# Where the shared expert's two halves run, and in which PSUM banks, in an attention and mixture-of-experts kernel

## The chip, the cores and the metric

One Trainium2 chip, one of its cores. The metric is the device time of one execution in microseconds; lower is better. Times of the kernel before: median 366.74 us of three runs (364.2 to 368.2).

## The reference

The input is x, 8 batches of 128 tokens of width 256, in float32. First x is normalised, goes through cross attention (16 query heads, 4 key and value heads, width 128, RMS norms and rotary turns, a context of 128 tokens ahead of the causal part), and the result is added to x. Then the second part, which the change is about:

```python
xt = layernorm(x).reshape(-1, 256)                    # 1024 tokens
scores = sigmoid(xt @ gate.T)                         # 8 experts
_, sel = top_k(scores + expert_bias, 2)
# for each token and each of its two experts e, in bf16:
#   xb = xt * score;  h = silu(xb @ w1[e].T) * (xb @ w3[e].T);  out_r = h @ w2[e].T
hs = silu(xt @ shared_w1.T) * (xt @ shared_w3.T)      # the shared expert, float32
out = hs @ shared_w2.T                                # plus the out_r of both experts
x = x + out
```

## The kernel before

The work is written by hand for five queues: SyncE (`sync`), ScalarE (`scalar`), GpSimd (`gpsimd`), VectorE (`vector`) and TensorE (`tensor`). Each has a block of code in its own order and waits on semaphores for the others. The order on each queue is the order of the code; no scheduler moves anything.

The attention runs over 8 batches x 4 groups of heads (`row`), the first and the last batch written out and a loop between. It takes from the start to 317.60 us. In its last batch it already turns the gate's and the shared expert's weights (`turn_down_gate`, `turn_shared`) and the normalised tokens of the first batches (`turn_xn2`, L1373), and forms the gate's logits of the first half (`logits(0)`). It ends with the output product in four quarters (`out_quarter`).

The expert stage works on two halves n of 4 batches (512 tokens) with 8 experts each, so 16 steps k, of which k = 0 to 7 belong to the first half. It is dense: each expert works on all 512 tokens, and `weight` (the score, or zero where the expert isn't among the token's two) scales the tokens first. One step k is:

- scaling: ScalarE takes one batch (`e_scale`, L657), VectorE one (L1119), GpSimd two (L852). All write to `xb[k % 4]`. ScalarE and VectorE are LEAD = 5 steps ahead.
- SyncE waits for all three and issues a transposing DMA to `xbT[k % 6]` (L443 to L448). A scaling of step k waits until the transpose of step k - 4 has landed. The names of these buffers in the trace are those of older ones whose room they take: wq, k_sum, k_rot for xb; wq, k_t, kc_n, q_t for xbT; wk for hid_e.
- up (`expert_up`, L1475): four matmuls of TensorE, 128x512, into two PSUM banks, one for w1 and one for w3.
- ScalarE's Silu of the first bank (`e_act`, L664), VectorE's product with the second (`e_hidden`, L1126).
- down (`expert_down`, L1487): four matmuls that add to the two banks `proj`, which hold the half's output.

The shared expert does the same for a half at once, in float32 from `xn2T`: up (`shared_up`, L1495) of eight matmul passes, Silu (L681), product (L1149), down (`shared_down`, L1507). Its down product starts the sum in `proj`. After a half, VectorE adds `proj` to x in two pieces (L1161) and SyncE writes the output out (L452). Behind the first half's first step the logits of the second half are formed (`logits(1)`), ScalarE takes their exponential (`gate_exp(1)`, L652) and VectorE turns them into weights (`router(1, ...)`, L1094), in pieces between the hidden products.

PSUM has eight banks here: `proj` (two), `turn`, `sc_ps` (two, as `sc_a` and `sc_b`), `pt_ps` (two) and `o_ps`. Two pairs serve the up products in turn:

```python
up_pairs = ((sc_a, pt_ps[:, 0, :]), (sc_b, pt_ps[:, 1, :]))
def up_banks(k):
    return up_pairs[(k + k // E) % 2]
def shared_banks(n):
    return up_pairs[(n + 1) % 2]
```

So the shared up takes a turn in the same two pairs, and the experts' up products around it wait for its pair to come free.

ScalarE loads a function table where the function changes: Exp, used in the attention and for the gate, and Silu are in different ones; copies need none.

## Time and profile before

| | us |
|---|---|
| median of 3 runs | 366.74 (364.2 to 368.2) |
| the profiled execution | 366.01 |
| its span, first to last instruction | 364.3 |
| TensorE busy | 329.9 (91%) |
| VectorE busy | 316.9 (87%) |
| ScalarE busy | 263.7 (72%) |
| GpSimd busy | 166.5 (46%) |

PE is TensorE's matmuls, PEld its weight loads, DVE is VectorE, ACT is ScalarE, POOL is GpSimd, SPq the queue of SyncE. The mean granted clock of TensorE was 0.989 of full speed. All times of rows are microseconds from the start of the span. In the order of time the first column is the start, the second how long it took; in square brackets stands how long the engine was idle before, and what ended that.

### The profile page before, as it was taken

The page shows a single profiled execution, that of the slowest core. Times are in us where ns is not written, and L with a number is a line of the kernel's source. Part 1 is how long each engine was busy: PE and PEld are TensorE (multiplying, and loading weights), DVE is VectorE, ACT ScalarE, POOL GpSimd, SP SyncE. Part 2 cuts the span into 40 slices and gives each one's busy share as a digit, 9 for nine tenths or more (in the row PEclk, how much of TensorE's full clock was granted, in tenths as well). Part 3 has the DMA queues.
Part 4 walks back from the last instruction along what each step waited for, and adds up shares of the span by engine and source line. Part 5 has one row for each costly group of instructions (what it writes and reads, how often), then busy time and mean ns, then how long its engine had stood idle before and what let it go on. Part 6 is the DMA issues. An engine that isn't in the chain of part 4 may idle for free.

```text
span 364.3 us, 7426 instructions
## 1 busy us (share of the span) xinstructions
PE 329.9 (91%) x2296; PEld 223.4 (61%) x2296; DVE 316.9 (87%) x602; ACT 263.7 (72%) x916; POOL 166.5 (46%) x241
## 2 busy tenths in 40 slices
PE   6788698799999999999999999999999999987894
PEld 6365455376667666866576657565856687754351
DVE  1779999998999899989999998999899987967643
ACT  3668989576986798679768976897599748447341
POOL 4467656652755175427532734263426230362600
PEclk9899989999999999999999999999999999999999
DMA  6977000000042005200300000000000000167844
GB/s 177 380 238 230 18 0 2 1 2 14 1 126 47 14 0 128 45 14 3 58 6 8 0 0 14 0 0 0 0 0 0 3 0 0 23 123 75 159 75 129
DMA packets 34835, 19.25 MB, mean 53 GB/s; under 512 B 24056, under 2 KB 32256, under 8 KB 34816
## 3 DMA queue, kind: packets, MB, share of 16 engines
q1 hardware_dynamic: 34816, 19.02, 20.6%
q8 instruction: 9, 0.15, 0.2%
q14 instruction: 10, 0.08, 0.1%
HBM read 12.20 MB, written 1.05 MB: 36 GB/s over the span
## 4 chain that ended last, share of the span: by engine, by line
PE 35%; DVE 24%; ACT 18%; issue 10%; POOL 6%; DMA 3%; SPq 1%; DVEq 1%; ACTq 0%; POOLq 0%
PE proj L1352 10%; ACT probs L549 7%; DVE probs L982 5%; PE pt_ps L1315 5%; PE turn L1261 3%; DVE nmax L970 3%; POOL q_rot L772 3%; PE o_ps L1325 3%; DVE pT_lo L908 3%; PE proj L1172 3%; PE sc_ps L1282 3%; ACT pT_hi L460 2%; DVE q_t L899 2%; ACT kc_junk L493 2%; DMA wq<-in_L_xattn_wq_dram 2%
## 5 line engine op out<-in xcount | busy, mean ns | idle before, releaser
L549 ACT ACTIVATE probs<-sc_ps,nbias,q_r 128x256 f32<-128x256 f32 x128 | 70.8, 573 | 2.8 <-DVE nbias L974 2.8
L772 POOL TENSOR_TENSOR q_rot<-q_t 128x512 f32<-128x512 f32 x32 | 42.4, 1325 | 41.3 <-DVE q_t L901 40.5
L982 DVE TENSOR_SCALAR probs<-probs,rden 128x256 f32<-128x256 f32 x128 | 51.2, 461 | 1.1
L460 ACT ACTIVATE pT_hi<-pt_ps 128x512 f16<-128x512 f32 x64 | 34.8, 597 | 10.1 <-PE pt_ps L1315 10.1
L493 ACT ACTIVATE q_junk<-proj 128x128 bf16<-128x128 f32 x128 | 34.0, 294 | 10.8 <-DVE q_t L901 10.8
L1172 PE MATMUL proj<-wq_hi,xT 128*128 128x512 f16 x128 | 39.2, 389 | 2.1 <-DVE wq_lo L892 2.1
L908 DVE SCALAR_TENSOR_TENSOR pT_lo<-pt_ps,pT_hi 128x512 f16<-128x512 f32 x64 | 40.9, 680 | 0.1
L970 DVE TENSOR_REDUCE nmax<-sc_ps 128x4 f32<-128x1024 f32 x32 | 38.8, 1214 | 1.5 <-PE sc_ps L1304 1.5
L729 POOL TENSOR_TENSOR q_r<-q_me,power 128x4 f32<-128x4 f32 x32 | 33.4, 1044 | 2.5
L460 ACT ACTIVATE qT_hi<-turn 128x512 f16<-128x512 f32 x32 | 19.5, 610 | 20.5 <-PE turn L1261 20.5
L1315 PE MATMUL pt_ps<-ident,probs 128*128 128x128 f32 x256 | 34.1, 277 | 0.2
L1352 PE MATMUL proj<-wo_hi,oT_hi 128*128 128x256 f16 x112 | 30.5, 273 | 0.0
L1352 PE MATMUL proj<-wo_lo,oT_hi 128*128 128x256 f16 x112 | 30.5, 273 | 0.0
L1352 PE MATMUL proj<-wo_hi,oT_lo 128*128 128x256 f16 x112 | 30.5, 273 | 0.0
L1315 PEld LDWEIGHTS pt_ps<-ident,probs 128*128 128x128 f32 x256 | 29.4, 143 | 0.6 <-DVE probs L982 0.3
L1261 PE MATMUL turn<-ident,q_rot 128*128 128x128 f32 x128 | 19.8, 278 | 10.9 <-POOL q_rot L772 5.3
L493 ACT ACTIVATION_READ_ACCUMULATOR q_junk<-proj 128x1 f32 x128 | 28.5, 226 | 0.0
L549 ACT ACTIVATION_READ_ACCUMULATOR probs<-sc_ps,nbias,q_r 128x1 f32 x128 | 27.5, 215 | 0.0
L1325 PE MATMUL o_ps<-pT_hi,v_hi 128*128 128x512 f16 x64 | 24.3, 379 | 2.8 <-DVE pT_lo L908 2.8
L908 DVE SCALAR_TENSOR_TENSOR oT_lo<-o_ps,oT_hi 128x512 f16<-128x512 f32 x32 | 21.9, 685 | 5.4 <-ACT oT_hi L460 5.4
L460 ACT ACTIVATE oT_hi<-o_ps 128x512 f16<-128x512 f32 x32 | 19.6, 613 | 7.8 <-PE o_ps L1325 7.8
L1282 PE MATMUL sc_ps<-kT_hi,qT_hi 128*128 128x256 f16 x128 | 24.5, 273 | 0.5 <-ACT probs L549 0.2
(221 smaller groups left out, 882.8 us busy)
## 6 DMA issues: line engine op xcount, KB each, us to landing
wq<-in_L_xattn_wq_dram SPq DMA_DIRECT2D x4, 512.0 KB, 8.4
w<-in_L_ffn_w_dram SPq DMA_DIRECT2D x2, 1024.0 KB, 9.9
wq<-in_L_xattn_wo_dram SPq DMA_DIRECT2D x1, 2048.0 KB, 8.2
ctx_b<-in_ctx_dram SPq DMA_DIRECT2D x8, 128.0 KB, 2.0
out_dram<-x_all SPq DMA_DIRECT2D x4, 256.0 KB, 2.2
x_all<-in_x_dram SPq DMA_DIRECT2D x1, 896.0 KB, 12.0
wkc<-in_L_xattn_wk_ctx_dram SPq DMA_DIRECT2D x1, 512.0 KB, 3.9
wk<-in_L_xattn_wk_dram SPq DMA_DIRECT2D x1, 512.0 KB, 4.9
```

The costliest lines, as they stand in the source:

```text
L460: return nc.scalar.activation(out_, in_, ACT.Copy, scale=scale)
L493: last = nc.scalar.activation(junk[:, head], bank[:, head], ACT.Square, scale=scale, accum_out=dst[:, h:h + 1])
L549: last = nc.scalar.activation(probs[:, h, :], sc_ps[:, h, :], ACT.Exp, bias=nbias[:, h:h + 1], scale=q_r[:, g, h:h + 1], accum_out=den[:, ...
L772: nc.gpsimd.tensor_tensor(q_rot[:], q_t1[:], q_t2[:], ALU.add).then_inc(q_added, 1)
L908: return nc.vector.scalar_tensor_tensor(out=lo, in0=src, scalar=scale, in1=hi, op0=ALU.mult, op1=ALU.subtract)
L970: nc.vector.tensor_reduce(nmax[:], sc_ps[:], AX_X, ALU.max, negate=True).then_inc(s_max, 1)
L982: last = nc.vector.tensor_scalar(probs[:, h, :], probs[:, h, :], rden[:, h:h + 1], None, ALU.mult)
L1172: last = nc.tensor.matmul(bank[:], xT[:, a, c, :], w[:, c, cols], start=(n == 0), stop=(n == 3 * DC - 1))
L1282: nc.tensor.matmul(sc_ps[:, h, :], a[:, h * P:(h + 1) * P], w[:, g, :, :].rearrange("p a t -> p (a t)"), start=start, stop=False, skip_gro ...
L1315: last = nc.tensor.transpose(pt_ps[:, a, h * P:(h + 1) * P], probs[:, h, a * P:(a + 1) * P], ident[:])
L1325: last = nc.tensor.matmul(o_ps[:], v[:, a, g * P:(g + 1) * P], p[:, a, :], start=(a == 0 and i == 0), stop=(a == 1 and i == 2))
L1352: last = nc.tensor.matmul(proj[0][:, 0:D], o[:, h // R, (h % R) * P:(h % R + 1) * P], w[:, h, :], start=(h == 0 and i == 0), stop=(h == H ...
```

## The change

A third pair of banks, `o_ps` and `turn`, serves the shared expert alone; the experts' pairs alternate by k without a break. The logits of the second half go to `turn` in place of `o_ps`, the turned tokens of the last two batches to `sc_b` in place of `turn`. On TensorE the second half's shared up moves from behind the up product of expert 7 to behind that of expert 3 (step k = 3), and the second half's shared down behind the up product of step 9. The up products run two steps ahead of the downs across the border of the halves too. On ScalarE a one-column activation loads Silu's table ahead of the last attention output's copy; the fifth scaling goes behind the shared Silu, and from then on each step's Silu is followed by its scaling, also in steps 0 and 1. On VectorE the fifth scaling goes behind the shared product. GpSimd waits for the last second norm before its fourth scaling, not its ninth. A semaphore `y_down` tells each of the two `proj` banks done by itself, and the second shared down waits for each add by itself.

TensorE, from the end of the attention's output product on; o_ps, turn, sc_ps and pt_ps are banks, sh13T the shared up weights, sh2T the shared down weights. Before:

```order
L1503 MATMUL sc_ps<-xn2T,sh13T 128x512 [waits r_sh13,p_ready]
L1503 MATMUL sc_ps<-xn2T,sh13T 128x512
L1503 MATMUL pt_ps<-xn2T,sh13T 128x512 x2
L1378 MATMUL turn<-ident,xn_all 128x128 [waits l2_done,r_sh13]
L1378 MATMUL turn<-ident,xn_all 128x128 x3
L1483 MATMUL sc_ps<-wq,w1T 128x512 [waits d_xbT0,n_ready2,d_wT]
L1483 MATMUL sc_ps<-wq,w1T 128x512
L1483 MATMUL pt_ps<-wq,w3T 128x512 x2
L1515 MATMUL proj<-sh2T,wq 128x256 [waits sh_hid,g_exp,x1_ready]
L1515 MATMUL proj<-sh2T,wq 128x256 x3
L1483 MATMUL sc_ps<-wq,w1T 128x512 [waits sh_hid,d_xbT1]
```

and now:

```order
L1514 MATMUL o_ps<-xn2T,sh13T 128x512 [waits r_sh13]
L1514 MATMUL o_ps<-xn2T,sh13T 128x512
L1514 MATMUL turn<-xn2T,sh13T 128x512 x2
L1493 MATMUL sc_ps<-wq,w1T 128x512 [waits d_xbT0,n_ready2,d_wT,p_ready]
L1493 MATMUL sc_ps<-wq,w1T 128x512
L1493 MATMUL pt_ps<-wq,w3T 128x512 x2
L1388 MATMUL sc_ps<-ident,xn_all 128x128 [waits l2_done,s_exp]
L1388 MATMUL sc_ps<-ident,xn_all 128x128 x3
L1527 MATMUL proj<-sh2T,wq 128x256 [waits sh_hid,g_exp,x1_ready]
L1527 MATMUL proj<-sh2T,wq 128x256 x3
L1493 MATMUL sc_ps<-wq,w1T 128x512 [waits n_ready3,d_xbT1]
```

The four turns and expert 0's up have changed places, and expert 1's up no longer waits for the shared product (`sh_hid`) but for the turned tokens (`n_ready3`), whose bank it takes.

TensorE, the steps around expert 3's up and expert 2's down. Before:

```order
L1483 MATMUL sc_ps<-k_t,w1T 128x512 [waits e_hid,d_xbT3]
L1483 MATMUL sc_ps<-k_t,w1T 128x512
L1483 MATMUL pt_ps<-k_t,w3T 128x512 x2
L1490 MATMUL proj<-w2T,wk 128x256 [waits e_hid]
L1490 MATMUL proj<-w2T,wk 128x256 x3
L1483 MATMUL sc_ps<-kc_n,w1T 128x512 [waits e_hid,d_xbT4]
```

and now:

```order
L1493 MATMUL sc_ps<-k_t,w1T 128x512 [waits e_hid,d_xbT3]
L1493 MATMUL sc_ps<-k_t,w1T 128x512
L1493 MATMUL pt_ps<-k_t,w3T 128x512 x2
L1514 MATMUL o_ps<-xn2T,sh13T 128x512 x2
L1514 MATMUL turn<-xn2T,sh13T 128x512 [waits g_exp]
L1514 MATMUL turn<-xn2T,sh13T 128x512
L1500 MATMUL proj<-w2T,wk 128x256 [waits e_hid]
L1500 MATMUL proj<-w2T,wk 128x256 x3
L1493 MATMUL sc_ps<-kc_n,w1T 128x512 [waits e_hid,d_xbT4]
```

The second half's shared up stands between expert 3's up and expert 2's down, and its second bank waits for the exponential of the second half's logits.

ScalarE, around the shared Silu of the first half and the two table loads of the gate. The rows with weight are scalings, those with o_ps or sc_ps to wq are Silus. Before:

```order
L460 ACTIVATE wq<-xn_all,weight 128x2x128 [waits d_xbT0,g_weight]
L681 ACT_TABLE_LOAD
L681 ACTIVATE wq<-sc_ps 128x512 [waits sh_up]
L460 ACTIVATE xn2T<-turn 128x2x256 [waits n_turned3]
L668 ACTIVATE wq<-sc_ps 128x512 [waits e_up] x2
L654 ACT_TABLE_LOAD
L654 ACTIVATE r_exp<-o_ps 128x32 [waits g_logit]
L460 ACTIVATE wq<-xn_all,weight 128x2x128 [waits d_xbT1,g_weight]
L668 ACT_TABLE_LOAD [waits e_hid]
L668 ACTIVATE wq<-sc_ps 128x512 [waits e_up]
```

and now:

```order
L682 ACTIVATE wq<-o_ps 128x512 [waits sh_up]
L459 ACTIVATE xn2T<-sc_ps 128x2x256 [waits n_turned3]
L459 ACTIVATE wq<-xn_all,weight 128x2x128 [waits d_xbT0,g_weight]
L667 ACTIVATE wq<-sc_ps 128x512 [waits e_up]
L459 ACTIVATE wq<-xn_all,weight 128x2x128 [waits d_xbT1,g_weight]
L667 ACTIVATE wq<-sc_ps 128x512 [waits e_up]
L459 ACTIVATE k_sum<-xn_all,weight 128x2x128 [waits d_xbT2,g_weight]
L653 ACT_TABLE_LOAD
L653 ACTIVATE r_exp<-turn 128x32 [waits g_logit]
L667 ACT_TABLE_LOAD [waits e_hid]
L667 ACTIVATE wq<-sc_ps 128x512 [waits e_up]
```

The first load has gone from here (it stands ahead of the attention's last copy), the fifth scaling has moved behind the shared Silu, and the scalings of experts 5 and 6 have moved ahead of the two loads of the gate.

The diff, cut to its core:

```diff
@@ ScalarE
             p_copy(G * B - 1)
+            nc.scalar.activation(warm[:], scale_x[:], ACT.Silu)
             o_copy(G * B - 1, G - 1)
-            for k in range(LEAD):
+            for k in range(LEAD - 1):
                 e_scale(k)
...
+            shared_silu(0)
+            xn_copy(3)
+            e_scale(LEAD - 1)
+            for k in range(E * NT):
+                e_act(k)
+                if k + LEAD < E * NT:
+                    e_scale(k + LEAD)
+                if k == 1:
                     gate_exp(1)
+                if k == 3:
+                    shared_silu(1)
@@ GpSimd
             l2_root(B - 1)
-            for k in range(3, E):
-                e_scale(k)
             pool.wait_ge(l2_done, B)
-            for k in range(E, E * NT):
+            for k in range(3, E * NT):
                 e_scale(k)
@@ VectorE
             def e_hidden(k):
                 dve.wait_ge(e_silu, k + 1)
-                seen(dve, e_down, k - 1)
+                seen(dve, e_down, k - 1 - (k - 1) // E)
...
+            def add_out(n):
                 for i in range(2):
+                    dve.wait_ge(y_down, 2 * n + i + 1)
...
+            shared_hidden(0)
+            e_scale(LEAD - 1)
+            for k in range(E * NT):
+                e_hidden(k)
+                if k == 1:
+                    router(1, 0)
+                if 1 <= k < 4:
+                    router(1, k)
+                if k == 3:
+                    shared_hidden(1)
+                if k + LEAD < E * NT:
+                    e_scale(k + LEAD)
+                if k % E == E - 1:
+                    add_out(k // E)
@@ TensorE
+            pe.wait_ge(r_sh13, 1)
+            shared_up(0)
             pe.wait_ge(p_ready, 2 * U)
-            shared_up(0)
-            turn_xn2(3, (r_sh13, 1))
             pe.wait_ge(d_wT, wT_landed)
...
+            expert_up(0)
+            turn_xn2(3, (s_exp, U))
+            shared_down(0)
+            expert_up(1)
+            logits(1)
+            expert_down(0)
+            expert_up(2)
+            expert_down(1)
+            expert_up(3)
+            shared_up(1)
+            for k in range(2, E - 1):
+                expert_down(k)
+                expert_up(k + 2)
+            expert_down(E - 1)
+            expert_up(E + 1)
+            shared_down(1)
+            for k in range(E, E * NT):
+                expert_down(k)
+                if k + 2 < E * NT:
+                    expert_up(k + 2)
```

## Rows read from the trace of the kernel before

**Rows 1.** The chain of waits: start us, us, what; in the expert stage

```profile
321.08 1.13 DVE k_rot L1124
322.21 1.05 DVE wq L1124
...
331.83 5.47 DMA wq<-k_sum
```

**Rows 2.** TensorE's matmuls in order of time, 317 us to the last

```profile
317.60 1.88 PE L1503 MATMUL sc_ps<-xn2T,sh13T 128*128 128x512 f32 x4
319.32 1.88 PE L1503 MATMUL pt_ps<-xn2T,sh13T 128*128 128x512 f32 x4
321.31 0.63 PE L1378 MATMUL turn<-ident,xn_all 128*128 128x128 f32 x4
321.77 0.59 PE L1483 MATMUL sc_ps<-wq,w1T 128*128 128x512 bf16 x2
...
324.01 1.97 PE L1515 MATMUL proj<-sh2T,wq 128*128 128x256 f32 x8 [1.21 <-DVE wq L1149]
325.81 0.59 PE L1483 MATMUL sc_ps<-wq,w1T 128*128 128x512 bf16 x2
...
326.67 1.85 PE L1387 MATMUL o_ps<-gateT,xn2T 128*128 128x8 f32 x16
328.38 0.60 PE L1490 MATMUL proj<-w2T,wk 128*128 128x256 bf16 x4
...
329.67 0.60 PE L1490 MATMUL proj<-w2T,wk 128*128 128x256 bf16 x4
...
332.06 0.61 PE L1490 MATMUL proj<-w2T,wk 128*128 128x256 bf16 x4 [0.93 <-DVE wk L1129]
...
349.02 0.60 PE L1490 MATMUL proj<-w2T,wk 128*128 128x256 bf16 x4
...
359.26 0.61 PE L1490 MATMUL proj<-w2T,wk 128*128 128x256 bf16 x4 [0.82 <-DVE wk L1129]
```

**Rows 3.** ScalarE in order of time, 311 to 330 us

```profile
311.87 1.08 ACT L460 ACTIVATE pT_hi<-pt_ps 128x512 f16<-128x512 f32 x2 [1.06 <-PE pt_ps L1315]
314.90 0.60 ACT L460 ACTIVATE oT_hi<-o_ps 128x512 f16<-128x512 f32 x1 [1.94 <-PE o_ps L1325]
...
320.47 1.28 ACT L681 ACT_TABLE_LOAD   x1
321.76 0.60 ACT L681 ACTIVATE wq<-sc_ps 128x512 f32<-128x512 f32 x1
...
328.88 0.50 ACT L460 ACTIVATE wq<-xn_all,weight 128x256 bf16<-128x256 f32 x1
329.39 1.28 ACT L668 ACT_TABLE_LOAD   x1
```

**Rows 4.** VectorE in order of time, 320 to 331 us

```profile
320.04 1.12 DVE L1003 TENSOR_SCALAR xn_all<-x_all,ln_mv,ln_rs 128x256 f32<-128x256 f32 x1 [0.76 <-POOL ln_rs L722]
...
323.18 0.68 DVE L1149 TENSOR_TENSOR wq<-pt_ps,wq 128x512 f32<-128x512 f32 x1
...
329.01 0.18 DVE L1100 TENSOR_SCALAR r_den<-r_exp 128x32 f32<-128x32 f32 x1 [0.82 <-ACT r_exp L654]
...
330.63 0.35 DVE L1124 TENSOR_SCALAR k_sum<-xn_all,weight 128x256 bf16<-128x256 f32 x1
```

**Rows 5.** GpSimd in order of time, its scalings beside VectorE's

```profile
320.97 2.14 POOL L859 TENSOR_TENSOR wq<-xn_all,weight 128x512 bf16<-128x512 f32 x2
```

**Rows 6.** A stretch (last columns: clock, DMA share, GB/s); DMA issues, us to landing

```profile
333.00:334.00 1.00, 0.69 (x5) 0.19 (x4) 1.00 (x3) 0.43 (x1) 0.00 (x0) 1.00 2.88 145
...
k_t<-wq SPq DMA_TRANSPOSE x2, 3.3
wq<-k_sum SPq DMA_TRANSPOSE x1, 5.5
wq<-k_rot SPq DMA_TRANSPOSE x1, 5.1
```

More of the change, by code:

```diff
@@ L674, in _, with shared_silu @@
             p_copy(G * B - 1)
+            nc.scalar.activation(warm[:], scale_x[:], ACT.Silu)
             o_copy(G * B - 1, G - 1)
-            for k in range(LEAD):
+            for k in range(LEAD - 1):
                 e_scale(k)
-            for n in range(NT):
+            def shared_silu(n):
                 act.wait_ge(sh_up, n + 1)
                 seen(act, sh_hid, n)
-                nc.scalar.activation(silu_s, shared_banks(n)[0], ACT.Silu).then_inc(sh_silu, 1)
-                if n == 0:
-                    xn_copy(3)
-                e_act(E * n)
-                if n == 0:
-                    e_act(1)
-                    gate_exp(1)
-                for k in range(E * n, E * (n + 1)):
-                    if k + 1 < E * (n + 1) and k:
-                        e_act(k + 1)
-                    if k + LEAD < E * NT:
-                        e_scale(k + LEAD)
+                nc.scalar.activation(silu_s, shared_banks[0], ACT.Silu).then_inc(sh_silu, 1)
+            shared_silu(0)
[6 more added lines that the diff above has]
+                if k == 1:
+                    gate_exp(1)
+                if k == 3:
+                    shared_silu(1)
         @block.gpsimd
@@ L1492, in expert_down @@
                                             stop=(k % E == E - 1 and t % 2 == 1), skip_group_check=True)
-                last.then_inc(e_down, 1)
+                    if k % E == E - 1 and t % 2 == 1:
+                        last.then_inc(y_down, 1)
+                if k % E < E - 1:
+                    last.then_inc(e_down, 1)
             def shared_up(n):
-                if n == 0:
-                    pe.wait_ge(r_sh13, 1)
-                else:
-                    pe.wait_ge(e_hid, E * n - 1)
-                for a, bank in enumerate(shared_banks(n)):
+                for a, bank in enumerate(shared_banks):
+                    if n and a:
+                        pe.wait_ge(g_exp, 2)
                     for c in range(DC):
```

44 lines of the change are left out of this document (12 added, 32 removed).

## The prediction

> **What bounds the kernel now.** I read the chain of waits first, then each engine's own order of time over the expert stage (317 us to the end), then the DMA view there. Everything up to 317.6 us is attention, is issued in the same order after the change and costs the same, with one exception on ScalarE (below).
>
> The chain [rows 1] shows that no single engine bounds the expert stage. It passes through VectorE's scalings at 321.08 and 322.21 and, later, one transposing DMA at 331.83 that takes 5.47 us. TensorE's own order [rows 2] gives its work: one half of the shared expert's up product 3.44 us (two banks of 1.72), its down product 1.80 (324.01 to 325.81), an expert's up 0.86 (325.81 to 326.67), the gate's logits 1.71 (326.67 to 328.38), and a down with an up 1.29 (328.38 to 329.67), so a down is 0.43. The four turns before the first expert take 0.46 (321.31 to the expert behind them). From 317.60 to the start of the last down product this is 2 x 3.44 + 16 x 0.86 + 15 x 0.43 + 0.46 + 2 x 1.80 + 1.71 = 32.9 us of work in 41.66 us: TensorE stands idle for 8.8 us. That idle time is what a reordering can win, and 350.5 us is the earliest start of the last down product.
>
> Even undisturbed, the experts don't run at 1.29 us. From the down product at 349.02 to the one at 359.26 there are seven, 1.46 us each [rows 2]. That is a latency: two experts share two bank pairs, and down 0.43, up with its tail 1.02, Silu 0.60, product on VectorE 0.69 and some 0.15 of signals make 2.9 us for two. The change leaves that loop as it is.
>
> **The change, part by part.**
>
> *Silu's table.* Before, the load (1.28) sits directly ahead of the shared Silu, which runs from 321.76 [rows 3]; its input is complete at 319.32 + 1.88 = 321.20 [rows 2]. Moved behind the copies that end at 311.87 + 1.08 = 312.95, the load and a one-column activation end by about 314.4, before the copy that waits until 314.90 [rows 3]. It costs nothing, hidden by that wait of 1.94 us. The shared Silu can then run 321.22 to 321.82.
>
> *Fifth scaling behind the shared product; GpSimd waits for the second norm.* Before, VectorE does two scalings of about 1.1 us between the norm and the shared product, which comes at 323.18; the norm itself takes 1.12 [rows 1, 4]. A scaling that GpSimd leaves alone takes 0.35 [rows 4]; beside GpSimd's scalings of 1.07 each [rows 5] they are as long as GpSimd's. Now GpSimd holds its fourth scaling back until the norm is done, so the norm should take about 0.4, and one scaling remains ahead of the product. Even if that one is held (to about 321.6) it is ready before the Silu. The product then runs 321.85 to 322.53, and TensorE, which took 0.15 us after it before, starts the shared down at 322.68 in place of 324.01. Its expert 0 and the four turns lie in 321.04 to 322.36, in front of it. **Gain 1.33 us.**
>
> *From there to the shared up of the second half.* No wait is left on TensorE: 322.68 + 1.80 + 0.86 + 1.71 = 327.05 for the first down (before 328.38), 328.34 for the second, 329.63 behind expert 3's up. Here 3.44 us of shared up product are put in, to 333.07. Its second bank waits for the gate's exponential. That one comes at: up of expert 1 complete 325.50, Silu to 326.1, one scaling 0.50, load 1.28, so about 327.9 to 328.1. The bank is wanted at 331.4, so the wait is free with 3.3 us to spare.
>
> What does the insertion hide? Expert 2's hidden product. ScalarE's second load now begins 0.1 us behind that exponential, at about 328.0, since the scaling that stood between them [rows 3] has moved ahead of the first. Silu 2 ends at 329.9. VectorE runs the router and its scaling in 1.62 + 0.35 us from 328.1 [rows 4], and expert 2's product in 330.1 to 330.8. Expert 3's follows by 332.6. Both are ready when TensorE asks for them at 333.07; before, it stood still for 0.93 us ahead of the down at 332.06 [rows 2], and again behind it.
>
> *The transposed tokens.* ScalarE's scalings for experts 5 and 6 now stand ahead of its second and third load. Expert 6's transpose then waits for VectorE alone and is issued at about 330.1, against 331.83 in the chain [rows 1]. Expert 6 is wanted at 337. With 3.3 us to landing it is there at 333.4, with 5.5 us at 335.6 [rows 6]. Either way the wait for this DMA goes. That long one isn't typical: in the microsecond from 333.00 the DMA engines' busy share reads 2.88 [rows 6], as packets begin there that stay open for long, and the two transposes around it took 5.5 and 5.1 us.
>
> *After the shared up.* Down of expert 2 at 333.07, up 4 at 333.50, down 3 at 334.36, up 5 at 334.79. The next down needs expert 4's hidden product: up complete 334.52, Silu to 335.14, product to 335.85. On VectorE in front of it stand the shared product and the scaling for the second half, 0.35 us alone and 1.05 beside GpSimd. The shared Silu can start at 333.25 and has at most one scaling (0.50) ahead of it, so the product ends by 335.0 and the held scaling by 336.1. So the down comes at 335.9 at best and 336.8 at worst. I take 336.6, since GpSimd starts its second-half scalings just then. Eleven periods of 1.46 bring the last down to 352.7. The second shared down adds 1.80 behind expert 9's up: the step there becomes 1.29 + 1.80 = 3.09 in place of 1.46, so 1.63 more: **354.3**, where it was 359.26.
>
> *Its new waits.* It asks for one add at a time. If VectorE is free, the first ends 0.4 + 0.65 us into expert 7's down, sooner than TensorE gets there (1.29): nothing. If a held scaling of 1.05 us stands in front, 0.46 us shows. I take nothing and keep 0.46 for the range. The added semaphore and the changed banks have no price in the rows; they add no instruction. At the end each add waits for its own bank, two of the four matmuls sooner: 0.22 us off the 5.04 from the last down to the end of the span.
>
> **Sum.** 354.3 + 4.8 = 359.1 us of span against 364.3, or 5.2 us less. The profiled execution took 366.01, 1.71 outside the span: 360.8. The median shown is 366.74, 0.73 above that execution: from it 361.5. I forecast 361.2 us, between them. TensorE's idle time falls from 8.8 to 3.8 us.
>
> **One rule against it.** The load's row ends at 321.75 and the Silu starts at 321.76 [rows 3], so 1.28 us is the whole price here. The Trainium skill ("ScalarE: Activation LUTs", What ACT_TABLE_LOAD costs) adds a drain of about 1.38 to a switch, 2.66 in all; the trace shows none behind this load. By that rule the moved load would end about 315.6.
>
> **The rivals.**
>
> *A. The second half is short of tokens.* Its first scaling on VectorE now stands behind the shared product, so expert 8's transpose is issued at about 336.0 and lands at 339.3 (3.3 us). It is wanted at 339.95, so the slack is 0.7. If a long one (5.5) falls here, 1.5 us is lost; with the held add, 2.0. For it: expert 7's was long too. Against: the two issued right behind it took 3.3 [rows 6]. Time 363.2.
>
> *B. The moved load reaches into the copy.* If the load occupied ScalarE beyond 314.90, the last attention output, the second norm and all behind it would shift. With an end at 315.6 that is 0.7 us: 361.9. The 0.01 us between load and Silu speaks against it.
>
> *C. Only the head gains.* The order promises that the 3.44 us fill idle time. If hidden products 2 and 3 are late for another reason, or VectorE's held scalings set the pace (0.60 + 1.05 = 1.65 a step over the eight steps of the second half, 1.5 us, and more where they meet the adds), TensorE gets the idle time back later and only the 1.3 us of the head stay: 365.4.
>
> *D. Slower: transposes of the second half pause in a row.* Place: SyncE's queue, experts 8 to 11. Each pause costs 5.5 - 3.2 = 2.3 us and delays the next, since the four token buffers are scaled again only after landing. Four cost 9.2, of which expert 11's slack takes 2.3: 6.9 more, 368.1. It decides from the fourth on, since three (4.6) don't eat the 5.2. Rows 6 show such a pause; nothing shows four.
>
> **How the numbers follow.** Forecast 0.64, its own range 359.5 to 362.8; A 0.17; B 0.05; C 0.10; D 0.04. Low end 358.8: no held scaling (0.7), a little of the waits covered by the second shared down, and the profiled run's account. High end 365.4 takes in A and C. A measurement of this kernel can tell about 1% from no change: faster means under 363.1. Forecast, B and part of A fall there, 0.77; the rest of A and C within 1%, 0.19; D slower, 0.04.
>
> **What would show it.** Right: one table load between 312.9 and 314.9; the shared product near 321.9 and the shared down's matmuls near 322.7; no idle time on TensorE from there to 333; no wait for expert 6's DMA; the down products of the second half 1.46 apart; the last at about 354.3. Wrong: a wait of ScalarE's copy behind the load (B), a DMA releaser ahead of expert 8 or 9 (A, D), VectorE's scalings ending TensorE's waits in most steps (C), or a long wait at the second shared down.

## The result and the profile after

The changed kernel takes 360.97 us (median of 4 executions, 360.24 to 362.27) against 365.82 us of the kernel before (4 executions, 364.2 to 368.2): a ratio of 0.9854 with a 95% interval of 0.9816 to 0.9893. By that ratio it is 5.3 us less; the two medians shown differ by 4.9. The whole interval lies more than 1% below the kernel before, and within 2% of it. A later set on another occasion (run e8 below) gave 0.9851. The forecast was 361.2 us. The profiled execution took 360.24 us, with a span of 357.6 us at a mean granted clock of 0.991, where before it had 364.3 at 0.989.

Below I call *the stage* the time from the start of the first shared up product to the start of the last down product on TensorE. It was 41.66 us before [rows 2] and is 35.60 us now. The work in it is the same 32.9 us, so TensorE's idle time there fell from 8.8 to 2.7 us. From the last down to the end of the span it is 4.80 us, before 5.04. Since these two give 6.3 us and the span is 6.7 us shorter, the other 0.4 us lie ahead of the stage, in attention that the change doesn't touch.

TensorE in order of time, changed kernel (start us, us, engine, line, operation, output<-inputs, count, and in brackets the idle time ahead with what ended it; a row without a bracket has no such wait, or one under about 0.15 us):

```profile
317.20 1.88 PE L1514 MATMUL o_ps<-xn2T,sh13T 128*128 128x512 f32 x4
...
322.30 1.97 PE L1527 MATMUL proj<-sh2T,wq 128*128 128x256 f32 x8 [0.21 <-DVE wq L1150]
...
329.27 1.88 PE L1514 MATMUL o_ps<-xn2T,sh13T 128*128 128x512 f32 x4
330.99 1.88 PE L1514 MATMUL turn<-xn2T,sh13T 128*128 128x512 f32 x4
332.70 0.60 PE L1500 MATMUL proj<-w2T,wk 128*128 128x256 bf16 x4
...
335.58 0.61 PE L1500 MATMUL proj<-w2T,wk 128*128 128x256 bf16 x4
...
336.89 0.60 PE L1500 MATMUL proj<-w2T,wk 128*128 128x256 bf16 x4
...
338.47 0.61 PE L1500 MATMUL proj<-w2T,wk 128*128 128x256 bf16 x4
...
341.08 1.92 PE L1527 MATMUL proj<-sh2T,wq 128*128 128x256 f32 x8
...
352.80 0.61 PE L1500 MATMUL proj<-w2T,wk 128*128 128x256 bf16 x4 [0.69 <-DVE wk L1129]
```

These rows answer to [rows 2]. The first shared down waits 0.21 us where it waited 1.21. The row at 332.70, expert 2's down, has no bracket, where the one before had 0.93 us: the two fp32 rows ahead of it (3.43 us of shared up of the second half) are what TensorE now does in that time. The second shared down (341.08) waits for nothing. The downs at 335.58, 336.89 and 338.47 are 1.31 and 1.58 us apart: two experts take 2.89 us, the latency loop that the change leaves as it is.

VectorE and GpSimd at the head of the stage, changed kernel:

```profile
319.64 0.41 DVE L1003 TENSOR_SCALAR xn_all<-x_all,ln_mv,ln_rs 128x256 f32<-128x256 f32 x1 [0.76 <-POOL ln_rs L724]
319.96 0.35 DVE L1124 TENSOR_SCALAR k_rot<-xn_all,weight 128x256 bf16<-128x256 f32 x1
321.46 0.69 DVE L1150 TENSOR_TENSOR wq<-turn,wq 128x512 f32<-128x512 f32 x1 [1.15 <-ACT wq L682]
...
320.13 1.08 POOL L861 TENSOR_TENSOR k_rot<-xn_all,weight 128x512 bf16<-128x512 f32 x1 [0.53 <-DVE xn_all L1003]
```

The norm takes 0.41 us in place of 1.12 [rows 4], the scaling behind it 0.35 in place of 1.13, and VectorE then stands still for 1.15 us until the shared Silu is done. GpSimd's bracket is the new wait: its scaling starts behind the norm. The shared product comes at 321.46, 4.26 us into the stage; before it came at 323.18, 5.58 us into it.

ScalarE, changed kernel:

```profile
312.57 1.28 ACT L674 ACT_TABLE_LOAD   x1
313.87 0.20 ACT L674 ACTIVATE warm<-scale_x 128x1 f32<-128x1 f32 x1
314.50 0.60 ACT L459 ACTIVATE oT_hi<-o_ps 128x512 f16<-128x512 f32 x1 [0.43 <-PE o_ps L1335]
...
320.83 0.60 ACT L682 ACTIVATE wq<-o_ps 128x512 f32<-128x512 f32 x1 [4.15 <-PE turn L1514]
...
327.69 1.28 ACT L667 ACT_TABLE_LOAD   x1
328.98 0.60 ACT L667 ACTIVATE wq<-sc_ps 128x512 f32<-128x512 f32 x1
```

The moved load sits in the wait for attention's last output, and 0.43 us of that wait remain of the 1.94 before [rows 3]. The one-column activation starts 0.02 us behind the load. But ScalarE also stands still for 4.15 us ahead of the shared Silu, which matters below (e2).

DMA issues of the changed kernel from 311 us on (output<-input, queue, operation, count, median us from issue to landing):

```profile
q_t<-wq SPq DMA_TRANSPOSE x1, 4.5
wq<-k_sum SPq DMA_TRANSPOSE x1, 3.0
wq<-k_rot SPq DMA_TRANSPOSE x1, 3.1
```

Experts 6 and 7 (the last two) land in 3.0 and 3.1 us, before in 5.5 and 5.1 [rows 6]; now expert 5's transpose is the long one, and nobody waits for it.

### The profile page after: what moved, and what is told of

Same layout as the page of the kernel before. It is cut to its first block, busy times and chain, and to the rows that moved or that the text cites. A ratio compares the mean times of both kernels' runs of the same rounds, so it can differ in the third digit from the quotient of the medians.

```text
span 357.6 us, 7425 instructions
## 1 busy us (share of the span) xinstructions
PE 326.2 (91%) x2292; PEld 222.8 (62%) x2296; DVE 313.5 (88%) x602; ACT 263.6 (74%) x917; POOL 166.4 (47%) x241
## 3 DMA queue, kind: packets, MB, share of 16 engines
HBM read 12.20 MB, written 1.05 MB: 37 GB/s over the span
## 4 chain that ended last, share of the span: by engine, by line
PE 37%; DVE 22%; ACT 19%; issue 11%; POOL 6%; DMA 2%; SPq 1%; DVEq 1%; ACTq 0%; POOLq 0%
PE proj L1362 10%; ACT probs L548 8%; PE pt_ps L1325 6%; DVE probs L982 6%; PE turn L1271 4%; POOL q_rot L774 3%; PE o_ps L1335 3%; DVE nmax L970 3%; DVE pT_lo L908 3%; PE proj L1182 3%; ACT pT_hi L459 3%; PE sc_ps L1292 3%; ACT kc_junk L492 2%; DVE q_t L899 2%; DMA wq<-in_L_xattn_wq_dram 2%
## 5 line engine op out<-in xcount | busy, mean ns | idle before, releaser
L1182 PE MATMUL proj<-wq_hi,xT 128*128 128x512 f16 x128 | 38.2, 380 | 2.7 <-DVE wq_lo L892 2.2
L1292 PE MATMUL sc_ps<-kT_lo,qT_hi 128*128 128x256 f16 x128 | 24.6, 273 | 0.0
```

The source lines that it names most:

```text
L1182: last = nc.tensor.matmul(bank[:], xT[:, a, c, :], w[:, c, cols], start=(n == 0), stop=(n == 3 * DC - 1))
L1292: nc.tensor.matmul(sc_ps[:, h, :], a[:, h * P:(h + 1) * P], w[:, g, :, :].rearrange("p a t -> p (a t)"), start=start, stop=False, skip_gro ...
```

## The experiments

Whole times scatter by about 0.5% from execution to execution, and what lies outside the stage took between 321.9 and 324.5 us in the profiles of kernels that do the same work there. The stage itself repeats: 41.66 and 41.61 us in two profiles of the kernel before, 35.60 and 35.59 in two of the changed one. So parts worth 1 or 2 us are told apart by the stage, and whole times serve as the second witness. Starts of the first shared down and of the down products, in us from the start of the stage:

| kernel | shared down | down 2 | down 3 | down 4 | down 5 | down 8 | last down |
|---|---|---|---|---|---|---|---|
| before | 6.41 | 14.46 | 16.24 | 17.78 | 20.63 | 31.42 | 41.66 |
| head only (e9) | 5.10 | 13.16 | 14.94 | 17.36 | 18.67 | 29.46 | 39.71 |
| shared up moved back (e1) | 5.11 | 13.17 | 14.95 | 17.37 | 18.68 | 28.51 | 38.46 |
| changed | 5.10 | 15.50 | 16.80 | 18.38 | 19.69 | 25.64 | 35.60 |

(The changed kernel's down 2 comes later since the 3.44 us of shared up stand ahead of it; in the others they are still to come.)

**e1, the place of the second shared up.** The changed kernel with that product, its Silu and its product put back behind expert 7's up; its own pair of banks stays.

```
...
-            shared_up(1)
             for k in range(2, E - 1):
                 expert_down(k)
                 expert_up(k + 2)
+                if k == 5:
+                    shared_up(1)
```

> The changed kernel with one thing undone: the second half's shared up goes back behind expert 7's up (its Silu and product on ScalarE and VectorE behind those of step 7), still in its own bank pair. I read the stage as the time from the start of the first shared up to the start of the last down: 41.66 us before, 35.60 in the changed kernel. Theory (the 3.44 us fill idle time while the table loads and the router hold experts 2 and 3): TensorE stands idle again ahead of the downs of experts 2 and 3, by about 1.0 and 1.3 us, and the shared up covers little where it now stands: stage 37.2 to 37.9, 2.0 us longer. Rival (the place doesn't matter, the third bank pair is what counts, since the shared up no longer waits for the experts' banks): stage 35.6 to 36.1.

363.51 us (10 executions), ratio 0.9924 (0.99 to 0.9947); stage 38.46 us, so the place is worth 2.86 us with all else as in the changed kernel. TensorE in that run:

```profile
331.92 0.61 PE L1500 MATMUL proj<-w2T,wk 128*128 128x256 bf16 x4 [0.93 <-DVE wk L1129]
...
333.70 0.61 PE L1500 MATMUL proj<-w2T,wk 128*128 128x256 bf16 x4 [0.30 <-DVE wk L1129]
...
336.12 0.61 PE L1500 MATMUL proj<-w2T,wk 128*128 128x256 bf16 x4 [0.95 <-DVE wk L1129]
...
345.46 1.97 PE L1527 MATMUL proj<-sh2T,wq 128*128 128x256 f32 x8 [0.53 <-DVE x_all L1156]
```

The four waits come back, 2.71 us of the 2.86: three for hidden products of experts 2, 3 and 4, and one for the add, as VectorE gets to it late. None of them is there in the changed kernel. The stage came out 0.6 us longer than the upper end of what I expected; the wait of 0.95 us, which the kernel before doesn't have in this form (its down 4 came 1.54 us behind down 3, here 2.42), is larger than that. Its cause is a held scaling on VectorE (shown under e9).

**e2, the early load.** The changed kernel without the one-column Silu.

```
-            nc.scalar.activation(warm[:], scale_x[:], ACT.Silu)
```

> The changed kernel without the one-column Silu, so that the table is loaded directly ahead of the shared Silu again. Theory (with the fifth scaling moved behind the shared Silu, ScalarE is idle for 4.15 us ahead of it, so the load lies there unseen): stage 35.6, the load from about 316.6 to 317.9, the shared Silu at its place. Rival (the load waits with its activation for the shared up, or the early load is a part of the gain): Silu and all behind it 0.6 to 1.3 us later, stage 36.2 to 36.9.

Stage 35.58 us (35.60 with it), 361.73 us in one execution. ScalarE in that run:

```profile
318.60 0.50 ACT L459 ACTIVATE k_rot<-xn_all,weight 128x256 bf16<-128x256 f32 x1
319.11 1.28 ACT L681 ACT_TABLE_LOAD   x1
323.24 0.60 ACT L681 ACTIVATE wq<-o_ps 128x512 f32<-128x512 f32 x1 [2.85 <-PE turn L1513]
```

The load isn't late without the edit: with the fifth scaling moved away, ScalarE comes to the load 4.13 us ahead of the Silu and stands still for 2.85 us behind it. The early load costs nothing and gains nothing in this order.

**e3, the head undone.** The changed kernel with the fifth scaling ahead again on ScalarE and VectorE, and GpSimd's wait undone.

```
-            for k in range(LEAD - 1):
+            for k in range(LEAD):
                 e_scale(k)
...
             xn_copy(3)
-            e_scale(LEAD - 1)
...
             e_scale(3)
+            e_scale(4)
...
             shared_hidden(0)
-            e_scale(LEAD - 1)
...
-            pool.wait_ge(l2_done, B)
-            for k in range(3, E * NT):
+            for k in range(3, E):
                 e_scale(k)
+            pool.wait_ge(l2_done, B)
+            for k in range(E, E * NT):
+                e_scale(k)
```

> The changed kernel with the fifth scaling ahead of the shared Silu and product again on ScalarE and VectorE, and with GpSimd's fourth scaling no longer waiting for the last second norm; the early table load stays. Theory (the head's gain is VectorE's: norm and two scalings held by GpSimd ahead of the shared product): norm about 1.1 us, two scalings about 1.1 each, shared product at about 322.9 instead of 321.46, the first shared down about 1.35 us later, and since everything behind it hangs on it, stage 36.9 to 37.0. Rival (the table load was what held the shared product before; the scalings only filled the wait): the first shared down at its place, stage 35.6. Second rival: the head comes late but is caught up where the second shared up covers waits: head 1.35 late, stage 35.6 to 36.2.

362.04 us (10 executions), ratio 0.9886 (0.985 to 0.9921); stage 36.93 us, with the shared down at 6.40 us. The norm takes 1.12 us again, the two scalings 1.13 each, and TensorE waits 1.50 us for the shared product. The head is worth 1.33 us, and of the 1.30 us at the first shared down nothing is lost up to the last down.

**e11 and e12, the two halves of the head.** e11 undoes only GpSimd's wait, e12 only the move of the fifth scaling (on ScalarE as in e3, too).

```
e11:
-            pool.wait_ge(l2_done, B)
-            for k in range(3, E * NT):
+            for k in range(3, E):
                 e_scale(k)
+            pool.wait_ge(l2_done, B)
+            for k in range(E, E * NT):
+                e_scale(k)
e12:
             e_scale(3)
+            e_scale(4)
...
             shared_hidden(0)
-            e_scale(LEAD - 1)
```

> The changed kernel with GpSimd's fourth scaling no longer waiting for the last second norm; the fifth scaling stays behind the shared product. With both undone the first shared down came at 6.40 us after the first shared up, with both in place at 5.10. Theory (each of the two moves takes one held instruction of about 1.1 us off VectorE's way to the shared product, and the Silu sets a floor): norm about 1.1 us again, one scaling held, shared product about 0.35 us later than in the changed kernel: head 5.4 to 5.5, stage 35.9 to 36.0. Rival (GpSimd's wait is the whole head): head 6.4, stage 36.9.

> The changed kernel with the fifth scaling ahead of the shared Silu and the shared product again on ScalarE and VectorE; GpSimd's wait for the last second norm stays. Theory (the norm then runs alone in 0.4 us and the two scalings, one of them held to about 1.1 us, end before the shared Silu does): head 5.10 to 5.15, stage 35.6. Rival (the fifth scaling's place is the whole head): head 6.2 to 6.4, stage 36.7 to 36.9.

e11: 361.88 us, stage 35.89 us, shared down at 5.36 us. e12: 360.18 us, stage 35.59 us, shared down at 5.10 us (one execution each). VectorE in e12:

```profile
320.13 0.41 DVE L1002 TENSOR_SCALAR xn_all<-x_all,ln_mv,ln_rs 128x256 f32<-128x256 f32 x1 [0.76 <-POOL ln_rs L723]
320.46 0.35 DVE L1123 TENSOR_SCALAR k_rot<-xn_all,weight 128x256 bf16<-128x256 f32 x1
320.72 1.13 DVE L1123 TENSOR_SCALAR wq<-xn_all,weight 128x256 bf16<-128x256 f32 x1
```

With GpSimd held back, norm and first scaling take 0.76 us together, and the second scaling, though held to 1.13 us, ends at 321.85 us, before the shared Silu does (321.93). So GpSimd's wait alone gives the whole 1.31 us, and the move of the scaling alone 1.05 us. They don't add, as 1.31 us is all that there was: behind it TensorE waits for ScalarE's Silu and not for VectorE.

**e9, the head alone, in the kernel before.** The kernel before with the early load, the fifth scaling behind the shared product, and GpSimd's wait.

```
+            nc.scalar.activation(warm[:], scale_x[:], ACT.Silu)
-            for k in range(LEAD):
+            for k in range(LEAD - 1):
                 e_scale(k)
...
                     xn_copy(3)
+                    e_scale(LEAD - 1)
...
-            for k in range(3, E):
-                e_scale(k)
             pool.wait_ge(l2_done, B)
-            for k in range(E, E * NT):
+            for k in range(3, E * NT):
...
-            e_scale(4)
...
+                if n == 0:
+                    e_scale(LEAD - 1)
```

> The kernel before with the head of the change alone: Silu's table loaded ahead of the last attention copy, the fifth scaling behind the shared Silu and the shared product, GpSimd's fourth scaling behind the last second norm. Banks, TensorE's order and the rest stay. Theory (the head's 1.31 us are its own and nothing takes them back): first shared down 5.10 us after the first shared up instead of 6.41, stage (first shared up to last down) 40.3 if a code fetch still falls into the transposes of experts 6 and 7, 38.9 to 39.1 if it has moved off them. Rival (in the old order with its one bank pair shared, the head is caught up at the next wait of the experts): stage 41.2 to 41.7 with the head at 5.10.

Stage 39.71 us, shared down at 5.10 us: 1.95 us less than before, between the two numbers expected: 40.3, and 38.9 to 39.1 if the pause had left expert 6's transpose, as it has here. 1.31 us of it is the head. The rest, 0.64 us, is what is left of TensorE's 1.3 us wait for expert 6's transpose, which is gone (it landed in 3.3 us), with a new wait of 0.95 us ahead of expert 4's down against it and smaller ones gone. The new wait is one scaling on VectorE. In e9 and in the kernel before:

```profile
333.41 1.24 DVE L1124 TENSOR_SCALAR wq<-xn_all,weight 128x256 bf16<-128x256 f32 x1
```

```profile
334.38 0.35 DVE L1124 TENSOR_SCALAR wq<-xn_all,weight 128x256 bf16<-128x256 f32 x1
```

In the kernel before it starts 0.10 us ahead of GpSimd's (334.48 us) and takes 0.35 us; in e9 it starts 0.04 us ahead of GpSimd's, by the trace, and takes 1.24, and expert 4's down comes 0.89 us later than before, counted from the first shared down. In e1 it is the same. In the changed kernel this scaling stands behind the shared product and takes 0.60.

The whole time doesn't show the 1.95 us: 365.96 us (10 executions) against 366.53 (17), ratio 0.9982 (0.9958 to 1.0007), where 1.95 us would be 0.9947. The profile is of one execution, at 365.11 us the second fastest of the ten; whether the long transpose comes back in others (the place of a pause isn't fixed, e5 below) I can't tell. That stays open.

**e4, the kernel before again.** No edit.

> The kernel before, unchanged, profiled once more, for the long transposes of experts 6 and 7 (5.5 and 5.1 us where others take 3.2). Theory (the pause belongs to that execution or to a code fetch that falls beside them by chance): expert 6 lands in 3.2 to 3.5 us, no wait of TensorE for it, stage about 40.3 (1.35 shorter), so that up to 1.4 of the 6.1 us between the two profiles is not the change's. Rival (it belongs to the program's place, and comes each time): 5.5 us again, stage 41.7.

367.85 us, stage 41.61 us. Its DMA issues from 318 us on and TensorE's row behind them:

```profile
wq<-k_sum SPq DMA_TRANSPOSE x1, 5.4
wq<-k_rot SPq DMA_TRANSPOSE x1, 5.0
```

```profile
339.19 0.61 PE L1483 MATMUL sc_ps<-wq,w1T 128*128 128x512 bf16 x2 [1.31 <-DMA wq<-k_sum]
```

I had said of the 5.5 us of expert 6 [rows 6] that they aren't typical. In this kernel they are: the same two experts take as long again, and TensorE waits 1.31 us for it again. That theory fell, and the rival held, that the pause comes again in this kernel.

**e5, the pause shifted.** In the stretch from 333 to 334 us of the kernel before, the DMA queues read:

```profile
q1 hardware_dynamic: 503, 0.13, 277.8%
q8 instruction: 1, 0.02, 10.0%
```

(queue and kind: packets, MB, share of time). One packet of an instruction queue, 16 KB of code, falls among the packets of a transpose, and 19 of these then stay open for more than 1 us, up to 1.96 (the busy share of 2.88 in [rows 6]). If that is the cause, the place depends on how many instructions stand ahead, and any instructions added far up should shift it. So the kernel before got 32 idle matmuls near 12 us:

```
             k(0)
+            keep_warm(32)
             pe.wait_ge(w_lo, 2)
             q(0, 0)
```

> The kernel before with 32 more of its one-bank filler matmuls, put where TensorE waits 2.11 us for VectorE near 12 us, so that TensorE's instruction stream is 64 instructions longer ahead of the expert stage; nothing in the stage is changed. In both profiles of the kernel before a 16 KB code fetch (queue 8) stands at 333.4 us of the first and at the same place of the second, some 20 data packets then stay open for up to 1.9 us, and the transposes of experts 6 and 7 take 5.4 to 5.5 and 5.0 to 5.1 us; in the other profiles the fetch falls elsewhere and none takes over 4.5. Theory (a code fetch that falls into a running transpose stalls it; where it falls is set by how long the streams are): the fetch moves, experts 6 and 7 land in 3.0 to 3.5, TensorE's wait of 1.35 us goes, stage (first shared up to last down) 40.2 to 40.4. Rival (the queue 8 fetch isn't TensorE's, or the stall belongs to this place of the order, whatever is fetched): again 5.4 and 5.0, stage 41.6.

369.91 us, stage 41.84 us. Issues from 318 us on:

```profile
kc_n<-wq SPq DMA_TRANSPOSE x1, 4.7
...
wq<-k_sum SPq DMA_TRANSPOSE x1, 3.4
wq<-k_rot SPq DMA_TRANSPOSE x1, 3.6
```

and TensorE, 36.5 us into the stage where e4's wait was 19.7 us into it:

```profile
357.81 0.61 PE L1484 MATMUL sc_ps<-wq,w1T 128*128 128x512 bf16 x2 [1.53 <-DMA wq<-wq]
```

The pause left experts 6 and 7 and came to expert 4, which has slack, and to experts 13 and 14 of the second half (5.2 and 4.7 us), of which 13 has none: down 5 came at 19.13 us in place of 20.63, and the 1.5 us were given back at the new place. The fetches are there too, one between 329.0 and 329.5 us (400 data packets around it, 4.7 us for that transpose) and one between 353 and 354. In the changed kernel the one fetch of 16 KB lies between 326.5 and 327 us, in expert 5's transpose (4.5 us). In e1 and e7 it falls into expert 5's too (4.5 and 4.7 us). In e3, e6, e8, e9, e11 and e12 it lies between two transposes, in e2 and e10 it starts 0.2 us before expert 5's lands, and in these eight none took over 3.9 us. The place isn't quite fixed by the order either: it lies 15.5 us into the stage in both profiles of the kernel before, but 9.5 us in the changed one and about 11 in the same kernel again (e8), where it misses. That all transposes over 4 us coincide with a 16 KB packet is what the 14 traces show; which engine's code is fetched, and why open packets stop for it, they don't. A second instruction queue (q14) brings three packets of 8 KB in every stage, and these fall among the packets of transposes too, without such a pause: in the stage of all 14 profiles, every data packet that is open for over 1 us starts within 0.8 us behind a 16 KB packet of q8.

**e6, ScalarE's scalings behind the loads again.** The changed kernel with ScalarE's scalings of experts 5 and 6 behind the gate's exponential and its load, as before.

```
-            for k in range(E * NT):
-                e_act(k)
-                if k + LEAD < E * NT:
+            e_act(0)
+            e_act(1)
+            gate_exp(1)
+            for k in range(E * NT):
+                if k > 1:
+                    e_act(k)
+                if k == 2:
+                    e_scale(6)
+                if k + LEAD < E * NT and k != 1:
                     e_scale(k + LEAD)
```

> The changed kernel with ScalarE's scalings of experts 5 and 6 behind the gate's exponential and its loads again, as before: Silu 0, Silu 1, load, exponential, scaling 5, load, Silu 2, scaling 6, scaling 7. My prediction's step gave this order a term: 0.5 us of scaling between exponential and load, so Silu 2 by 0.4 later. Theory now: the shared up hides it, since expert 2's product ends 2.4 us ahead of its down in the changed kernel, and the first load starts 0.5 us sooner without a scaling ahead of it: Silu 2 within 0.2 us of its place, stage 35.5 to 35.7. Rival (the order of scalings is what fed expert 5 and 6 in time): a DMA ends a wait of TensorE ahead of expert 5 or 6, stage 36.0 or more.

360.25 us, stage 35.59 us: no difference. The Silu of expert 2 starts 11.78 us into the stage in both.

**e7, a third pair for the experts.** The changed kernel, where from expert 10 on the shared pair of banks serves as a third one and ups run three ahead of downs.

```
-            return up_pairs[k % 2]
+            return up_pairs[k % 2] if k < E + 2 else (up_pairs + (shared_banks,))[(k - E) % 3]
...
             shared_down(1)
+            expert_up(E + 2)
             for k in range(E, E * NT):
                 expert_down(k)
-                if k + 2 < E * NT:
-                    expert_up(k + 2)
+                if k + 3 < E * NT:
+                    expert_up(k + 3)
```

> The changed kernel carried on: once the shared expert's second half has left its bank pair, the experts use it as a third one. From expert 10 on an up runs three steps ahead of its down and waits for the product three steps back. Theory (from 335.6 us on the changed kernel is bound by the loop down, up, Silu, product over two bank pairs, 1.42 us a step, against 1.30 of matmuls): the downs from 8 to 15 come 1.30 us apart instead of 1.42, the last down 1.0 us sooner, stage 34.5 to 34.7, all of it seen at the end. Rival A (VectorE, which reads PSUM in the product and scales beside GpSimd, or the landing of the tokens takes over): steps of 1.4 again, stage 35.3 to 35.7, with DMA or VectorE ending the waits ahead of the ups. Rival B (hid_e and silu_e have only two buffers, so the product waits for the down two steps back): stage 35.3 to 35.7 with VectorE waiting for downs.

359.43 us (6 executions), ratio 0.9827 (0.9794 to 0.9859); stage 34.84 us, 0.76 less than the changed kernel. The downs of the second half are now 1.30 us apart, TensorE's own pace, but for one step of 1.55 us:

```profile
344.87 0.60 PE L1502 MATMUL proj<-w2T,wk 128*128 128x256 bf16 x4
...
346.17 0.60 PE L1502 MATMUL proj<-w2T,wk 128*128 128x256 bf16 x4
...
347.47 0.60 PE L1502 MATMUL proj<-w2T,wk 128*128 128x256 bf16 x4
348.14 0.60 PE L1495 MATMUL sc_ps<-k_t,w1T 128*128 128x512 bf16 x2
```

So the 1.42 to 1.46 us of a step were the latency of two pairs and no engine's work. Between the third row and the fourth stand 0.67 us in place of 0.43: at the faster pace tokens become the next limit, and TensorE's weight load waits 0.4 us for one transpose.

**e8, the changed kernel again.** No edit.

> The changed kernel itself, on the same chip as the three pairs: to see how well the stage repeats and where the transposes land. Theory: stage 35.60 within 0.1, the transpose of expert 5 at 3.1 or 4.5 us and no wait for it, ratio to the kernel before 0.983 to 0.988.

360.62 us (6 executions), ratio 0.9851 (0.9815 to 0.9887); stage 35.59 us.

**e10, more supply ahead of the border.** The third pair from expert 6 on, up 6 ahead of down 4, VectorE's scalings for experts 8 and 9 earlier.

```
-            return up_pairs[k % 2]
+            return up_pairs[k % 2] if k < 6 else (up_pairs + (shared_banks,))[(k - 4) % 3]
...
-            for k in range(2, E - 1):
-                expert_down(k)
-                expert_up(k + 2)
-            expert_down(E - 1)
-            expert_up(E + 1)
+            expert_down(2)
+            expert_up(4)
+            expert_down(3)
+            expert_up(5)
+            expert_up(6)
+            expert_down(4)
+            expert_up(7)
+            expert_down(5)
+            expert_up(8)
+            expert_down(6)
+            expert_down(7)
+            expert_up(9)
             shared_down(1)
+            expert_up(10)
...
+                if k + LEAD < E * NT and k != 4:
+                    e_scale(k + LEAD)
                 if k == 3:
                     shared_hidden(1)
-                if k + LEAD < E * NT:
-                    e_scale(k + LEAD)
+                    e_scale(9)
```

> The three pairs carried further: the experts take the third pair from expert 6 on, right after the shared expert's second half has left it, the up of expert 6 stands ahead of the down of expert 4, and VectorE scales expert 8 ahead of the shared product and expert 9 ahead of expert 4's product, so that their transposes are issued sooner (about 334 and 335.3 instead of 334.9 and 336.2). Theory (what is left of TensorE's waits between 333 and 341 is half the bank loop, half the tokens of experts 8 and 9): second shared down about 0.6 us sooner than with three pairs alone, stage 34.1 to 34.4. Rival (moving the scalings ahead makes the shared product and expert 4's late, or expert 10's tokens come too late for the earlier place): stage 34.7 to 35.2, with VectorE or a DMA ending the waits.

359.33 us (6 executions), ratio 0.9805 (0.9773 to 0.9838); stage 34.17 us, the shortest of all. TensorE's waits from 323 us on:

```profile
PE proj L1503 <- DVE wk L1129: 0.5, 1, 0.5
PE proj L1530 <- DVE wq L1150: 0.2, 1, 0.2
```

(us in total, times, longest). Two waits of that size are left: the 0.2 us ahead of the first shared down, and the one ahead of the last down, which has no other work in front of it. Against e7 the medians differ by less than they scatter; only the stage (0.67 us) tells them apart.

## Why the prediction was right

The 6.06 us of the stage close as a ladder of single profiles: the head and its company 1.95 us (before to e9), the rest of the new order with its own banks 1.25 us (e9 to e1), the place of the second shared up 2.86 us (e1 to the changed kernel). The whole times bear out the last rung: 0.9924 against 0.9851 is 2.7 us. For the head behind it, 0.9886 (e3) against 0.9851 is 1.3 us, but the intervals overlap, so that its size rests on the stage. The first rung they don't bear out: e9's whole time gives 0.7 us, at most 1.5, and e9 against e1 then 2.1 in place of 1.25. So how the first 3.2 us divide is open. And part of the 6.06 us is a wait of the kernel before that needs no new order to go: in e5, where the pause had left expert 6, down 8 came 1.5 us sooner.

- *Silu's table, at no cost:* right. And there was no gain either: the shared Silu starts at 320.83 us, 321.23 in the frame of before, where I had 321.22, but e2 shows that moving the fifth scaling had already freed ScalarE for the load. Rival B is out: behind three loads (at 312.57, at 327.69, and at 320.47 in [rows 3]) the next activation starts 0.01 or 0.02 us later. The drain of 1.38 us that the Trainium skill ("ScalarE: Activation LUTs", What ACT_TABLE_LOAD costs) adds to a switch doesn't show here.
- *The head, 1.33 us:* right, 1.31 in the changed kernel and 1.33 by e3. I had both edits at work; e12 shows that GpSimd's wait does it alone, and e11 that the moved scaling alone gives 1.05 us.
- *The shared up fills waits:* right. Shifted by the 0.40 us that the stage starts earlier, expert 2's down stands at 333.10 us where I had 333.07. The bank that waits for the exponential is free: the exponential runs at 327.47 and the bank is written from 330.99. ScalarE's new order, to which I had given a part in the early tokens and Silus, does nothing (e6).
- *Expert 6's transpose stops mattering:* right in outcome; the step "That long one isn't typical" failed. The pause came again in the kernel before (e4), and moved when 32 matmuls were put ahead (e5). In the changed kernel the fetch fell to expert 5, which has slack, or between two transposes (e8), with the same stage. The slack that I had worked out (a landing at 335.6 even with 5.5 us, for 337) would have covered it as well, by an estimate from the changed kernel's rows: expert 6's transpose is issued at 329.71 us, with 5.5 us it would land at 335.2, and its up starts at 336.03. No profile has the pause there in the new order.
- *Expert 4's down:* mis-sized. I had it at 336.6 us with a held scaling of 1.05 us in front; it came at 335.58, in the same frame 335.98. VectorE's rows:

```profile
333.69 0.69 DVE L1150 TENSOR_TENSOR wq<-turn,wq 128x512 f32<-128x512 f32 x1 [1.06 <-ACT wq L682]
334.30 0.60 DVE L1124 TENSOR_SCALAR wq<-xn_all,weight 128x256 bf16<-128x256 f32 x1
334.83 0.69 DVE L1129 TENSOR_TENSOR wk<-pt_ps,wq 128x512 bf16<-128x512 f32 x1
```

  The held scaling took 0.60 us: GpSimd's operation beside it had started at about 333.7 and was 0.6 us in. A held scaling ends 0.15 us behind GpSimd's, in all 14 traces, so holding costs what is left of the other engine's operation, and I had taken the whole. The Trainium skill ("SBUF — State Buffer", Who interferes with whom) has a rule like it for VectorE's two-port modes, that whoever issues first keeps the shared ports for its whole instruction and the other blocks. The trace agrees, with 0.60 us here and 1.13 where GpSimd's had started 0.1 us before, and in the other direction too: at 338.33 us VectorE's starts first and takes 0.34 us, and GpSimd's at 338.40 takes 1.18 in place of 1.04. Which mode the scaling runs in, no row shows.
- *Eleven periods of 1.46 and 1.63 for the shared down:* a little too long. Down 4 to down 7 took 4.20 us (1.40 a step), the step with the shared down 3.06 (I had 3.09), and the last seven 9.96 (1.42 a step): 17.22 in place of 17.69. The seven steps of before that I had taken, 10.24 us, hold 0.3 us more than the same seven now. With the 0.62 of the term above that is 1.09 us, the whole error of the last down: in the frame of before it stands at 353.2, not 354.3.
- *Idle time:* 2.7 us and not 3.8, the same 1.1 us.
- *The new waits at nothing:* right, the first add starts at 340.20 us behind 0.23 us of idle time, and the second shared down waits for nothing. The tail is 0.24 us shorter (I had 0.22).

Rival A (tokens short in the second half) fell in the changed kernel, where no DMA ends a wait of TensorE. Its slack was real and as small as I had it: expert 8's transpose lands at 338.26 us, and its up starts at 338.92. And e5 shows the mechanism: one pause, at an expert without slack, costs 1.53 us. Rival C (only the head gains) fell, since 2.86 us are the place alone. Rival D (pauses in a row) has nothing for it: one fetch lengthens two transposes in a row (5.5 and 5.1 us, in e5 5.2 and 4.7), no profile shows more, and the two fetches of e5 came 24 us apart. That the forecast of 361.2 us met 360.97 so closely is in part luck: the stage gained 1.1 us more than the sum had, and the whole times show less (5.3 us by the ratio, 4.9 by the medians) than the spans of the two profiled executions (6.7 us), which scatter by more than a microsecond outside the stage.

What I can't split further: the 1.25 us between e9 and e1, which hold the own pair of banks, the order at the border between the halves and the separate adds together. e9 waits 1.21 us at its second shared down, where e1 waits 0.53; no run takes the banks alone.

## What to carry to other kernels

Where a loop waits on other engines, here at its start, on the gate's two table loads, its router and a held scaling, independent matmuls belong into these waits: moving 3.44 us of them there won 2.86 us. I read the extra pair of banks as worth most where it lets such work move; no run takes it alone. Before adding up several edits, ask what stands behind the wait that each removes: here the early load was worth nothing once a scaling had moved, and of the head's two edits one alone gave the whole. And before calling an odd duration chance, profile the same kernel once more.

## What the runs showed of the hardware

- A transpose of a bf16 128x1024 tile takes 3.0 to 3.9 us from issue to landing, and 4.5 to 5.5 where a 16 KB packet of an instruction queue falls among its packets (10 transposes, in the stages of 6 of the 14 profiles). The 8 KB packets of the other instruction queue had no such effect. With 32 matmuls added some 320 us earlier it came to expert 4 and one of the second half in place of experts 6 and 7. So an edit far from a wait can move about 1.5 us.
- VectorE's scaling of 128x256 takes 0.35 us alone. Where GpSimd's of about 1.07 us has begun before it and still needs more than 0.2 us, VectorE's ends 0.15 us behind that one, so it takes up to 1.13 us. Where it starts 0.04 us ahead of GpSimd's it took 1.24 in some cases and 0.34 in others.
- Two pairs of banks run the expert loop at 1.42 to 1.46 us a step, three at 1.30.
